# Reordering the steps of a software pipeline on four engines of one core

## The reference

```python
x0 = layernorm(x)
gf = global_net(x0.mean(axis=1))          # one number per batch: two gelu layers, sigmoid
out = x0
for _ in range(3):
    tf = coupling_net(out)                # 256 -> 256 -> 128 -> 64 -> 1, three gelus, sigmoid
    coupling = 0.1 + adaptive_range * (0.7 * gf + 0.3 * tf - 0.5) * 2.0
    out = out + coupling * twist(out)     # twist permutes and negates four blocks of 64 features
x = x + out
```

## Time and profile before

| | |
|---|---|
| median of 3 runs | 894.32 us (893.6 to 894.84) |
| the profiled execution | 893.9 us |
| its span, first to last instruction | 892.4 us |
| busy share of the span | PE 88%, PEld 72%, DVE 81%, ACT 52%, POOL 41% |
| mean granted TensorE clock | 0.928 |
| first transposes of phase two | at 510.3 us |
| last `scale` of phase two (L237) | at 822.6 us |

### The profile page before, as it was taken

The page is one execution under the profiler, slowest core; times in us unless marked ns, Lnnn a source line. Parts: engine busy times, 40 slices in busy tenths (PEclk is TensorE's granted clock), DMA queues, the critical chain, the costliest instruction groups (busy, mean ns, idle before and its releaser), DMA issues. The chain is left out here.

```text
span 892.4 us, 13579 instructions
## 1 busy us (share of the span) xinstructions
PE 782.7 (88%) x4240; PEld 638.8 (72%) x4240; DVE 720.0 (81%) x1695; ACT 463.6 (52%) x1020; POOL 365.0 (41%) x375
## 2 busy tenths in 40 slices
PE   4679999999999999999999789888888979898952
PEld 3568888888887888888888666666666757675731
DVE  5879898998998989979988737786977696868675
ACT  2445665556565665565656346554544454445431
POOL 3536634564266345642560014343433333333331
PEclk9899999999999999999999989988988797979775
DMA  6000011001100110011000080000100010101011
GB/s 193 1 1 19 30 49 48 18 31 48 48 25 25 48 48 24 25 48 48 1 1 1 18 265 1 21 27 15 35 24 14 11 48 1 44 5 48 1 48 48
DMA packets 34570, 32.43 MB, mean 36 GB/s; under 512 B 3524, under 2 KB 34244, under 8 KB 34500
## 3 DMA queue, kind: packets, MB, share of 16 engines
q1 hardware_dynamic: 34500, 31.56, 11.1%
HBM read 16.88 MB, written 14.68 MB: 35 GB/s over the span
## 5 line engine op out<-in xcount | busy, mean ns | idle before, releaser
L507 ACT ACTIVATE pT_hi<-bank 128x512 fp32r<-128x512 f32 x192 | 91.2, 492 | 98.7 <-PE bank L846 90.5
L554 ACT ACTIVATE x_all<-scores_ps,neg_max 128x384 f32<-128x384 f32 (+7 forms) x128 | 94.7, 740 | 37.5 <-DVE neg_max L690 37.1
L581 DVE TENSOR_TENSOR pT_lo<-bank,pT_hi 128x512 fp32r<-128x512 f32 x192 | 100.7, 548 | 13.5 <-ACT pT_hi L507 12.4
L846 PE MATMUL bank<-ident,x_all 128*128 128x128 f32 x576 | 91.6, 276 | 20.3 <-DVE pT_lo L581 19.8
L690 DVE CUSTOM_DVE_ANT_0 scores_ps<-scores_ps,x 128x384 f32<-128x384 f32 (+7 forms) x128 | 96.6, 760 | 14.6 <-PE scores_ps L740 14.0
L1345 PE MATMUL cycle_ps<-h,w_sb 128*128 128x512 f32 x192 | 93.5, 624 | 12.5 <-ACT h L1111 12.5
L384 POOL TENSOR_TENSOR rope_a<-x_all,cos_sb 128x384 f32<-128x384 f32 x60 | 61.7, 1028 | 103.2 <-ACT x_all L507 98.9
L846 PEld LDWEIGHTS bank<-ident,x_all 128*128 128x128 f32 x576 | 67.7, 140 | 35.6 <-DVE pT_lo L581 26.3
L1060 POOL TENSOR_TENSOR h_w<-h,w_sb 128x256 f32<-128x256 f32 x48 | 36.5, 762 | 102.6 <-ACT h L1125 102.6
L738 PE MATMUL oT_ps<-pT_hi,v_hi 128*128 128x512 f32 x192 | 75.9, 395 | 1.3 <-issue 1.0
L1345 PEld LDWEIGHTS cycle_ps<-h,w_sb 128*128 128x128 f32 x192 | 36.4, 198 | 47.7 <-issue 25.2
(11 more groups left out here) (129 smaller groups left out, 2165.2 us busy)
## 6 DMA issues: line engine op xcount, KB each, us to landing
x_all<-x SPq DMA_DIRECT2D x16, 512.0 KB, 4.0
out<-x_all SPq DMA_DIRECT2D x16, 512.0 KB, 2.9
x<-x_all SPq DMA_DIRECT2D x12, 512.0 KB, 2.9
x_all<-x SPq DMA_DIRECT2D x6, 1024.0 KB, 7.2
x_all<-wqkv SPq DMA_DIRECT2D x1, 512.0 KB, 5.2
sin_sb<-sin_t SPq DMA_DIRECT2D x1, 512.0 KB, 7.0
cos_sb<-cos_t SPq DMA_DIRECT2D x1, 256.0 KB, 5.8
x_all<-wo SPq DMA_DIRECT2D x1, 256.0 KB, 5.4
```

The costliest lines, as they stand in the source:

```text
L507: return nc.scalar.activation(out, in_, ACT.Copy)
L554: nc.scalar.activation(probs[u % 2][:, k, 0:keys], scores_ps[k % 2][:, 0:keys], ACT.Exp, bias=neg_max[:, u * G + k:u * G + k + 1], scale=-1.0,
L581: return dve.tensor_tensor(out, whole, hi.bitcast(F32), ALU.subtract)
L846: mm = nc.tensor.transpose(ps[:, k * P:(k + 1) * P], probs[u % 2][:, k, j * P:(j + 1) * P], ident[:])
```

## The change

Four lists are replaced by others with the same steps; no instruction is added, removed or altered, and no wait, buffer or guard. To compare them each list has to be turned round to the same point and its offsets shifted, since a period may begin anywhere in the cycle. With group n as the group of `turn`, one period afterwards runs:

- PE: turn (n), h3 of cycle 0 (n-1), global 0 (n), h3 of cycle 2 (n-3), global 1 and global 2 (n), product 0 (n), spread 1 (n-1), spread 2 (n-2), products 1, 2 and 3 (n), h2 of cycles 0, 1, 2 (n, n-1, n-2), h3 of cycle 1 (n-1).
- ACT: turn, h3 of cycle 0, global 0, h3 of cycle 2, global 1, squash 1, squash 0, global 2, squash 2, products 0 and 1, gelu1 of cycles 0 and 1, products 2 and 3, gelu1 of cycle 2, h2 of cycles 1, 0, 2, h3 of cycle 1.
- DVE: turn, dot 1, dot 0, global 2, squash 0, dot 2, squash 1, squash 2, mix 1, mix 2, four finals, scale, stats. Before, dot 2 and squash 1 stood ahead of global 2 and squash 0; the rest is the same.
- POOL: mix 2, dot 1, dot 0, dot 2, stats, mix 1. Before: dot 0, stats, dot 1, dot 2, mix 1, mix 2.

The start now covers one period more and the end one period more, since the offsets reach from -4 to 2 and before from -3 to 1.

```diff
--- before.py
+++ after.py
@@ -876,27 +876,26 @@
 
 PERIODS = {
     "tensor": [
-        ("product", -1, 0), ("global", -1, 2), ("product", -1, 1), ("spread", -2, 1),
-        ("spread", -3, 2), ("product", -1, 2), ("h2", -1, 0), ("product", -1, 3), ("h3", -1, 0),
-        ("h2", -2, 1), ("h2", -3, 2), ("turn", 0, 0), ("turn", 0, 1), ("h3", -2, 1),
-        ("global", 0, 0), ("h3", -3, 2), ("global", 0, 1),
+        ("h2", -2, 0), ("h2", -3, 1), ("h2", -4, 2), ("h3", -3, 1), ("turn", -1, 0),
+        ("turn", -1, 1), ("h3", -2, 0), ("global", -1, 0), ("h3", -4, 2), ("global", -1, 1),
+        ("global", -1, 2), ("product", -1, 0), ("spread", -2, 1), ("spread", -3, 2),
+        ("product", -1, 1), ("product", -1, 2), ("product", -1, 3),
     ],
     "scalar": [
-        ("product", -1, 3), ("h3", -1, 0), ("h2", -2, 1), ("h2", -3, 2), ("turn", 0, 0),
-        ("turn", 0, 1), ("global", 0, 0), ("h3", -2, 1), ("h3", -3, 2), ("global", 0, 1),
-        ("squash", -2, 1), ("squash", -1, 0), ("global", 0, 2), ("squash", -3, 2),
-        ("product", 0, 0), ("product", 0, 1), ("gelu1", 0, 0), ("h2", 0, 0), ("gelu1", -1, 1),
-        ("product", 0, 2), ("gelu1", -2, 2),
+        ("product", 0, 0), ("product", 0, 1), ("gelu1", 0, 0), ("gelu1", -1, 1), ("product", 0, 2),
+        ("product", 0, 3), ("gelu1", -2, 2), ("h2", -1, 1), ("h2", 0, 0), ("h2", -2, 2),
+        ("h3", -1, 1), ("turn", 1, 0), ("turn", 1, 1), ("h3", 0, 0), ("global", 1, 0),
+        ("h3", -2, 2), ("global", 1, 1), ("squash", -1, 1), ("squash", 0, 0), ("global", 1, 2),
+        ("squash", -2, 2),
     ],
     "vector": [
-        ("scale", 0), ("stats", 1), ("turn", 0, 0), ("turn", 0, 1), ("dot", -2, 1), ("dot", -1, 0),
-        ("dot", -3, 2), ("squash", -2, 1), ("global", 0, 2), ("squash", -1, 0), ("squash", -3, 2),
-        ("mix", -1, 1), ("mix", -2, 2), ("final", -3, 0), ("final", -3, 1), ("final", -3, 2),
-        ("final", -3, 3),
+        ("turn", -1, 0), ("turn", -1, 1), ("dot", -3, 1), ("dot", -2, 0), ("global", -1, 2),
+        ("squash", -2, 0), ("dot", -4, 2), ("squash", -3, 1), ("squash", -4, 2), ("mix", -2, 1),
+        ("mix", -3, 2), ("final", -4, 0), ("final", -4, 1), ("final", -4, 2), ("final", -4, 3),
+        ("scale", 0), ("stats", 1),
     ],
     "gpsimd": [
-        ("dot", -1, 0), ("stats", 1), ("dot", -2, 1), ("dot", -3, 2), ("mix", -1, 1),
-        ("mix", -2, 2),
+        ("mix", -2, 2), ("dot", -1, 1), ("dot", 0, 0), ("dot", -2, 2), ("stats", 2), ("mix", 0, 1),
     ],
 }
 AHEAD = max(step[1] for steps in PERIODS.values() for step in steps)
```

## The result

The changed kernel takes 857.34 us (median of four runs, 856.72 to 859.27) against 894.58 before: a ratio of 0.959, 95% interval 0.957 to 0.961. The profiled execution took 856.72 us with a span of 854.5.

The account below looks back on a forecast made before the run. DVE was taken to bound full-clock periods, PE's slowed clock the long ones. Terms -9.6, -0.6, -6.1, -2.6, -3.7 and +0.7 sum to -21.9 from 893.9: 872.0, given as 872.5 us; range 859 to 893.

Parts of the forecast that it names:

- no fall at all: Rival on PE's clock: all six periods with global steps take 20.6 us, kernel 859 us; chance 0.08.
- I expect the fall to stay in five of six: Clock before periods with global steps: after a 1.6 us wait only one escapes the fall, -2.6 us.
- What bounds the kernel: Phase two: DVE sets full-clock periods (17.50 of 18.85 us busy); PE's 2.3 us wait is paid for later in clock.
- Product 1 and global 2: PE order before spread 1: `part_b` starts 1.6 us earlier in each of six low-clock periods with global steps, -9.6 us.
- h3: Cycles 0 and 1 exchanged around turn: L1207 gains 0.47 us, held L237 costs 0.35, together -0.1 per period.
- Rstd: POOL's rstd behind the three dots runs beside DVE's squashes: +0.25 us in a full-clock period.
- The rival in which POOL takes what PE gives: POOL's rstd and h_w hold DVE's squashes and L237, +1.25 us in each of 16 periods: 902 us; chance 0.11.
- PE's tail: PE's work after spread 2 grows to 10.5 us, so its wait before turn falls from 2.33 to about 1.6 us.
- First periods and end: Start of phase two: -2.4 us from earlier turn, -1.3 in the first period with global steps; end: +0.7.

Follow-up runs that it names:

- after_late_scale: Changed kernel with three unused bn_stats and a drain on DVE ahead of every scale, lengthening PE's wait; 901.93 us, ratio 1.009.
- before_filler: Kernel before the change, same order, with eight unused 512-column matmuls on PE ahead of the wait for turn from group 4 on; 860.48 us, ratio 0.966.
- after_stats_early: Changed kernel with DVE's stats moved ahead of the four finals, directly behind mix 2; 875.5 us, ratio 0.983.
- after_dve_back: Changed kernel with DVE's dot 2 and squash 1 ahead of global 2 and squash 0 again, as before; 851.36 us, ratio 0.953.
- after_filler: Changed kernel with five unused 512-column matmuls on PE ahead of the wait for turn from group 4 on; 861.82 us, ratio 0.963.
- after_h3_back: Changed kernel with h3 and dot of cycles 0 and 1 exchanged back on all four engines; 861.73 us, ratio 0.966.
- dve_back_tail_filler: Changed kernel with DVE's old order of dot 2 and squash 1, plus filler matmuls in four PE waits of the last three periods; 847.37 us, ratio 0.948.

## Why the prediction was wrong

The direction was right, and so were the parts that the change works through (PE's pause, the clock, the chain to `part_b`). The clock behind the shorter pause was forecast wrongly, and the size with it: 857.3 lies 1.7 us below the range and close to the rival "no fall at all" (859), which had a chance of 0.08. That its number is so near is in part luck: four of the five G periods still have a fall, and the periods without one are shorter than that rival took them (19.9 us for 20.6 with global steps, 17.9 to 18.3 for 19.0 without).

*The step that failed* is that of the clock: "I expect the fall to stay in five of six". The fall behind the pause stayed in none. No G period of the five begins at low clock; the falls that are left start some 5 us behind the first transpose, near product 0, and are shorter (3.4 us in three, 6.8 in one, against 10.2 in all five before). For these five periods the prediction had -1.7 each and -2.6 once more, -11.1; measured are -21.0. I took the light h3 next to the pause as a reason for the fall to stay; with a wait of 1.43 us it did not. after_late_scale shows that the shorter wait matters, and not only the new order: with 2.1 to 2.4 us before the G periods, and PE's order that of after, falls of 13.7 us directly behind it are back in four of five.

*What bounds the kernel.* That PE's pause has a price by the clock was right, and before_filler shows it: the old order, with PE kept busy, loses 31 us. That DVE sets the full-clock period was only half of it: after_stats_early takes 1.3 us of busy time from DVE and the period does not shrink. What sets it are the ways from scale to `part_b` and from there to the next scale.

*Product 1 and global 2.* The `part_b` at 12.6 us after scale was for G periods that start low, and there are none. The direct part is real, and more than the 9.6 us of the sum: taking product 1 back costs 15 us. The 0.4 us between global 1 and 2 is 0.41.

*h3.* The -0.47 of L1207 is there in full: as L1206 it takes 0.35 us, and from `part_b` to scale it is 10.24 to 10.34 us for 10.70. Only the G period at 633.60 has 10.73, since DVE waits 0.48 us for PE ahead of `part_a` there. The held L237 costs 0.41 in the G periods and the two of 18.3 us (scale 1.79 us for 1.38) and nothing in the four of 17.94, where the h_w comes after the scale; 0.35 was the forecast.

*Rstd.* The +0.25 was wrong. Six times each, L1162 (0.21 us), L1224 (0.29) and L1237 (0.16) ran inside rstd's 1.02 us at their usual lengths. L1237 is a `tensor_tensor` with both inputs in SBUF, the others are `tensor_scalar` of 128x1 and 128x4. So the rule of the Trainium skill (SBUF - State Buffer, Who interferes with whom), by which GpSimd can hold both kinds, does not show for them here, and the measurement decides; for L237, a `tensor_scalar` of 128x256 beside an h_w, it does (0.82 us for 0.41). The rival in which POOL takes what PE gives has no support. With dot 1 ready before turn, DVE also no longer waits for h_w ahead of its dots, which I had not counted; the way from scale to `part_b` became 0.46 us shorter in the four shortest periods (7.69 for 8.15), and not 0.25 longer. Together with h3 that makes the six periods without global steps -11.7 where -6.1 was forecast.

*PE's tail.* 1.6 us of pause before G periods and 0.5 to 1.2 behind them were forecast; it is 1.43 before them, and behind them 0 to 0.56 in four periods and 1.43 in two.

*First periods and end.* -3.7 became -1.2: the third scale is 1.9 us earlier, but after has a fall of 6.8 us at 527 that before had not, and by the fourth scale only 0.2 is left. The first G period gives 1.0 more. The end was to cost 0.7 and, with the last G period, to give 1.0 in all; it gives 4.0. The size that was wrong is again that of a G period without a fall behind the pause: its `part_b` comes 9.62 us after scale for 14.19, 4.6 less, where 1.7 was the forecast; what follows it costs 0.6.

*The shift.* That the new periods alone do nothing was taken for granted; 1.002 (0.998 to 1.006) agrees.

What is not settled: why the clock still falls late in some G periods, and why it does not in after_dve_back.

## What to carry to other kernels

When PE has slack, ask where it spends it: a single pause of 2.3 us ahead of light work cost up to 4.3 us of slow clock behind it (23.19 us for 18.85), and slack in two pieces of 0.6 and 0.9 us was followed by no fall. A few unused matmuls in the pause tell in one run what the clock is worth (31 us of 892 here), before any order is redesigned. And a change of four lists should be taken apart: one of its parts, DVE's new order, cost 6 us of what the rest gained.

## What the hardware did that was not expected

A step that was to give an engine time made the kernel slower twice: DVE's earlier squash 0 (857.3 against 851.4) and the early stats (875.5 against 857.3). Both times PE paused longer before turn (1.43 us for 0.6, 1.89 for 1.43). For the early stats the falls directly behind the pause came with it; for squash 0 the link is not shown, since after_filler fills that pause and gains nothing.

The longer the pause, the surer was a fall directly behind it, but the length does not settle it alone. Pauses of 0.2 to 0.8 us were never followed by one in the eleven periods of any kernel. Of the 46 of 1.4 to 1.6 us one was, of 1.51 us in after_h3_back. All five of 1.89 us stood before G periods, and four were followed by a fall of 10.2 or 13.7 us within 1.6 us. Pauses of 2.33 us were followed by one of 10.2 us before every G period, and before the others by 10.2, by 3.4 or by none, in the same kernel and the same order. Through a fall of 10.2 us in the kernel before PE never paused.

How many falls a run has can vary, too: in the session of 13 runs the mean clock of before lies between 0.924 and 0.940 and its time between 881.6 and 897.2 us, while in the first session four runs of it lie within 1.4. The four runs each of after_dve_back and dve_back_tail_filler lie within 2.5 and 1.4.
